# The expert stage of a graph and mixture-of-experts kernel, with TensorE's work cut into steps of one kind and two signals each

## What is computed

```python
h = (x_flat @ W_gat).reshape(M, HEADS, NUM_EXPERTS)
e = leaky_relu(a_src[src] + a_dst[dst], 0.2)
ee = exp(e - segment_max(e, dst)[dst])
agg = segment_sum(h[src] * (ee / segment_sum(ee, dst)[dst])[:, :, None], dst)
scores = layernorm(agg + b_gat).mean over heads
for ei in range(NUM_EXPERTS):            # 4
    g = weight of expert ei (softmax of the best two scores)
    hh = gelu(x @ W1[ei] + b1[ei])       # 256 -> 512
    out = out + g * (hh @ W2[ei] + b2[ei])  # 512 -> 256
```

## Time and profile before

| | us |
|---|---|
| median of 3 runs | 4049.74 (4045.44 to 4051.8) |
| the profiled execution | 4058.66, its span in the trace 4057.0 |
| PE busy over the span | 1940.2 (48%) |
| DVE busy | 1968.4 (49%) |
| ACT busy | 663.5 (16%) |
| GpSimd busy | 1737.6 (43%) |

### The profile page before, as it was taken

The page is one execution under the profiler, slowest core; times in us unless marked ns, Lnnn a source line. Parts: engine busy times, 40 slices in busy tenths (PEclk is TensorE's granted clock), DMA queues, the critical chain, the costliest instruction groups (busy, mean ns, idle before and its releaser), DMA issues.

```text
span 4057.0 us, 25978 instructions
## 1 busy us (share of the span) xinstructions
PE 1940.2 (48%) x7318; PEld 1438.6 (35%) x7322; DVE 1968.4 (49%) x3777; ACT 663.5 (16%) x1401; POOL 1737.6 (43%) x1787
## 2 busy tenths in 40 slices
PE   4415044444334353546541395554657565556425
PEld 3311033233223132324430374443546454444314
DVE  7876776645656653446520163233334343233646
ACT  7300021122112121212310011010101011011003
POOL 0015765655565444540777314344442424343241
PEclk9758566666666676767565697777878787777757
DMA  3211344544455343434621011111110111111415
GB/s 123 36 48 28 87 157 152 164 155 154 137 170 164 113 145 121 160 116 168 178 77 8 13 37 27 26 22 22 31 31 29 28 31 25 24 22 25 180 55 211
DMA packets 154183, 354.73 MB, mean 87 GB/s; under 512 B 55510, under 2 KB 96518, under 8 KB 144406
## 3 DMA queue, kind: packets, MB, share of 16 engines
q1 hardware_dynamic: 68303, 196.54, 13.5%
q0 software_dynamic: 69936, 121.07, 12.7%
q10 hardware_dynamic: 15866, 36.29, 2.3%
HBM read 181.01 MB, written 172.19 MB: 87 GB/s over the span
## 4 chain that ended last, share of the span: by engine, by line
PE 18%; another core or an unknown queue 16%; issue 10%; DVE 7%; ACT 1%; DMA 1%; POOL 0%; ACTq 0%; SPq 0%; DVEq 0%; POOLq 0%
PE ffn_psY L1512 7%; PE ffn_psH L1498 6%; PE pick_rows L858 3%; DVE pick_prod L888 1%; DVE at_ring L897 1%; DVE at_ring L692 1%; PE mid_psH L1424 1%; PE mid_psT L1181 1%; DVE pick_hot L874 0%; POOL acc L979 0%; DVE xnT L1715 0%; DVE at_high L662 0%; PE pick_node L839 0%; DVE at_ring L684 0%
## 5 line engine op out<-in xcount | busy, mean ns | idle before, releaser
L618 POOL DMA_INDIRECT at_ring<-table,e_col x768 | 725.9, 945 | 1061.2 <-DMA at_sums<-at_ring 831.2
L2057 POOL DMA_INDIRECT at_ring<-table,at_idx x693 | 671.9, 970 | 585.1 <-DMA at_sums<-at_ring 378.4
L2149 PE MATMUL at_psS<-at_ring,at_hot 128*128 128x260 f32 x1584 | 495.1, 475 | 437.4 <-issue 268.9
L1498 PE MATMUL ffn_psH<-xnT,ffn_space 128*128 x896 | 405.3, 605 | 452.5 <-ACT ffn_space L1539 289.4
L888 DVE SCALAR_TENSOR_TENSOR pick_prod<-const_iota,pick_tile,pick_rows 128x400 f32<-128x400 f16 x256 | 158.5, 629 | 831.1 <-remote 547.5
L2149 PEld LDWEIGHTS at_psS<-at_ring,at_hot 128*128 128x128 f32 x1584 | 346.9, 236 | 575.3 <-issue 351.3
L1512 PE MATMUL ffn_psY<-ffn_space 128*128 128x256 f32 x1568 | 387.7, 405 | 286.4 <-DVE ffn_space L1570 271.9
L1498 PEld LDWEIGHTS ffn_psH<-xnT,ffn_space 128*128 128x128 f32 x896 | 271.9, 312 | 553.8 <-ACT ffn_space L1539 301.0
L1512 PEld LDWEIGHTS ffn_psY<-ffn_space 128*128 128x128 f32 x1568 | 314.9, 204 | 345.8 <-DVE ffn_space L1570 285.8
L2171 ACT ACTIVATE at_ring<-at_psS 128x520 f32<-128x520 f32 (+1 forms) x432 | 238.7, 567 | 768.0 <-PE at_psS L2149 354.6
L1539 ACT ACTIVATE ffn_space<-ffn_psH,ffn_b 128x448 f32<-128x448 f32 x224 | 141.5, 634 | 1056.4 <-DMA at_sums<-at_ring 790.7
(11 more groups left out here) (404 smaller groups left out, 2432.6 us busy)
## 6 DMA issues: line engine op xcount, KB each, us to landing
at_sums<-at_ring SPq DMA_DIRECT2D x72, 1452.0 KB
products<-ffn_space ACTq DMA_DIRECT2D x28, 512.0 KB
at_ring<-table,e_col POOLq DMA_INDIRECT x867
at_sums<-at_ring SPq DMA_DIRECT2D x16, 768.0 KB, 3.2
late_space<-products SPq DMA_DIRECT2D x24, 512.0 KB, 7.9
at_ring<-table,at_idx POOLq DMA_INDIRECT x693
products<-ffn_space ACTq DMA_DIRECT2D x28, 384.0 KB
late_space<-products SPq DMA_DIRECT2D x24, 384.0 KB, 9.8
```

Of the source, the lines that this page charges most:

```text
L618: g.indirect_dma_start(self.ring[z][:, k, 0:TW], None, self.table, bass.IndirectOffsetOnAxis(ap=self.runs.col[:, u * U + k:u * U + k + 1], ...
L1498: last = pe.matmul(self.psH[part][:, 0:half], self.w1[:, k, e * HID + f:(e + 1) * HID:FT], self.xnT[:, k, bass.ds(r * (BT * P) + part * ha ...
L2057: g.indirect_dma_start(self.ring[z][:, k, 0:self.TW], None, self.table, bass.IndirectOffsetOnAxis(ap=self.idx[:, z, k:k + 1], axis=0)).the ...
L2149: last = pe.matmul(self.psS[at % 2][:, k - lo, 0:TW], self.hot[:, b, k, :], rows[:, b * self.SUB + k, 0:TW], start=True, stop=True)
```

## The change

PE's work in the stage is cut into 112 steps, 16 in a round. A step is one slice of the first layer (both parts), up to two tiles of the second layer (of the slice five steps behind, `LAG`), and two picked columns. The two tiles lie in one PSUM bank, and DVE adds the bias to both in one instruction. A step has two signals: `s_step`, on the last column, for DVE (tiles, columns and node spread together), and `s_hidden`, on the last part of the slice, for ACT. DVE does one step after one wait: `take` (mask both columns), `add`, `put` (one-hots, sum). `weigh` is cut in two pieces, placed at steps 5 and 6 for one unit and 11 and 13 for the other, `scores` at 3 and 10. The last five products of the network share their steps with further picks, and the last 5 chunks use four banks (`pick_rows` and `psH`) with one signal each. On SP, the loads of the next stage stand after the store of unit 13.

```diff
-    def column(self, pe, n, z, k, kept):
-        pe.wait_ge(self.s_kept, kept)
...
-        last.then_inc(self.s_out, 1)
+        for k in range(2):
+            pe.wait_ge(self.s_kept, r * self.ROUND + (slot * 2 + k + 1))
+            last = self.column(pe, self.ps_rows[k], i % 2, half * 2 + k)
+        return last
...
+    def hidden(self, pe, r, s):
+        e, f = divmod(s, FT)
+        for part in range(2):
+            pe.wait_ge(self.s_hid, r * (2 * self.STEPS) + (2 * s + part + 1))
...
+    def product(self, pe, r, n):
+        e, j = divmod(n % self.STEPS, FT)
+        lo, hi = self.PAIRS[j]
+        pe.wait_ge(self.s_prod, r * self.STEPS + (n + 1))
...
+        with pe.Fori(1, self.rounds) as r:
+            for s in range(self.STEPS):
+                self.product(pe, r, s - self.LAG)
+                picks(r, s).then_inc(self.s_step, 1)
+                self.hidden(pe, r, s).then_inc(self.s_hidden, 1)
...
+    def activate(self, a, r, s):
+        a.wait_ge(self.s_hidden, r * self.STEPS + (s + 1))
+        for part in range(2):
+            a.activation(self.hid[:, e % 2, f, part * half:(part + 1) * half], self.psH[part][:, 0:half],
...
+    def add(self, v, n):
+        if j % 2 == 0:
+            v.wait_ge(self.s_kept[j // 2], 16 * e + 16)
+        v.tensor_tensor(self.prod[:, lo:hi, :], self.psY[j % 2][:, 0:(hi - lo) * self.DIM].rearrange("p (t d) -> p t d", d=self.DIM),
...
-                        att.sync(sp, lambda: mix.begin(sp, ffn), ffn.rounds * 2 - 2)
+                        att.sync(sp, lambda: mix.begin(sp, ffn), ffn.rounds * 2)
...
+                        def step(i):
+                            v.wait_ge(ffn.s_step, i + 1)
+                            pick.take(v, i, pick.ps_rows)
+                            if 0 <= i - ffn.LAG < ffn.steps:
+                                ffn.add(v, i - ffn.LAG)
+                            pick.put(v, att, i)
```

More of the change, by code:

```diff
@@ L812, in table_vector @@
         v.wait_ge(self.s_att, 16)
+        v.wait_ge(self.s_node, 1)
         self.hots(v, 0)
@@ L875, in hots, with take, put @@
                 .then_inc(self.s_hot, 1)
-    def vector(self, v, att, slot):
-        q, S, D = self.q, self.SPAN, self.D
+    def take(self, v, slot, banks):
+        S, D = self.SPAN, self.D
+        tiles = self.c["iota16"][:, 0:S].unsqueeze(1).to_broadcast([P, D, S])
+        for k in range(2):
+            n = slot * 2 + k
+            v.scalar_tensor_tensor(out=self.prod[:, k, :, :], in0=tiles, scalar=self.tile[:, n:n + 1],
+                                   in1=banks[k][:, 0:S * D].rearrange("p (d s) -> p d s", d=D),
+                                   op0=ALU.is_equal, op1=ALU.mult).then_inc(self.s_kept, 1)
+    def put(self, v, att, slot):
+        q, D = self.q, self.D
         q.eng = v
@@ new lines, in hidden @@
+    def hidden(self, pe, r, s):
+        FT, K, BT, HID, half = self.FT, self.K, self.BT, self.HID, self.BT * P // 2
+        e, f = divmod(s, FT)
+        for part in range(2):
+            pe.wait_ge(self.s_hid, r * (2 * self.STEPS) + (2 * s + part + 1))
+            for k in range(K):
+                last = pe.matmul(self.psH[part][:, 0:half], self.w1[:, k, e * HID + f:(e + 1) * HID:FT],
+                                 self.xnT[:, k, bass.ds(r * (BT * P) + part * half, half)],
+                                 start=(k == 0), stop=(k == K - 1))
+        return last
@@ new lines, in product @@
+    def product(self, pe, r, n):
+        FT, DIM = self.FT, self.DIM
+        e, j = divmod(n % self.STEPS, FT)
+        lo, hi = self.PAIRS[j]
+        pe.wait_ge(self.s_prod, r * self.STEPS + (n + 1))
+        for t in range(lo, hi):
+            for f in range(FT):
+                last = pe.matmul(self.psY[j % 2][:, (t - lo) * DIM:(t - lo + 1) * DIM],
+                                 self.hid[:, e % 2, f, t * P:(t + 1) * P], self.w2[:, e * FT + f, :],
+                                 start=(f == 0), stop=(f == FT - 1))
+        return last
@@ new lines, in _ @@
+                        last = att.units - 1
+                        for i in range(ffn.steps, slots):
+                            step(i)
+                            if i == ffn.steps:
+                                att.scores(v, last - 2)
+                            if i == ffn.steps + 2:
+                                att.weigh_first(v, last - 2)
+                            if i == ffn.steps + 3:
+                                att.weigh_second(v, last - 2)
+                        chunks = range(slots // 2, pick.chunks)
@@ L2814, in _ @@
+                        for c in chunks:
+                            late_chunk(c)
+                            if c == chunks[1]:
+                                att.scores(v, last - 1)
+                            if c == chunks[2]:
+                                att.weigh(v, last - 1)
                         pick.end_vector(v)
@@ L2841, in _ @@
                         ffn.scalar(a, beside)
-                        for u in range(ffn.rounds * 2 - 1, att.units):
+                        for i in range(ffn.steps, ffn.steps + ffn.LAG + 1):
+                            ffn.store(a, 0, i - ffn.LAG - 1)
+                            if i == ffn.steps + 1:
+                                att.exponents(a, att.units - 3)
+                        for u in range(att.units - 2, att.units):
                             att.exponents(a, u)
@@ L2865, in _ @@
                     def _(pe):
-                        def between(r):
-                            pick.tensor(pe, r, next(slots))
                         join.tensor(pe)
```

235 lines of the change are left out of this document (106 added, 129 removed).

## The result

The changed kernel takes 3926.2 us (median of 4 runs, 3920.4 to 3938.2), the kernel before in the same session 4048.8: a ratio of 0.970 (95% interval 0.968 to 0.973). The forecast was 3770, with 3670 to 3900. The sign was right, and the gain is 123 us where 279 were forecast. The profiled execution took 3922.05 us, its span 3920.1.

A forecast was written before the change was run, and what follows sets the result against it. PE's signals, passing 11.2 us apart in GpSimd's gathers, were taken as the bound. Unit 3's gather at 2335 plus six rounds of 194, 56 + 73 to the last `weigh` and 149.4 gave a span of 3777, forecast 3770 us (3670 to 3900).

The forecast's parts named there:

- The bound now: Expert stage: during GpSimd's gathers PE's signals pass one at a time, in PE's order, 11.2 us each; a round takes 230.7 us.
- slow stretches: Part of each gather, from about 9 us after its start: 57 us with six signals passed, two in a round.
- a price for each signal: PE's hand-over to ACT and DVE during a gather: each signal costs 11.2 us, not a common delay.
- three places: Rival, expert-stage steps: each step takes three hand-over places, not two; a round is 209 us, the time 3895; chance 0.13.
- A round after: Expert-stage round: two stretches of 57 us pass 6 steps, the other 10 take 76, restarts 4: 194 us against 230.7.
- passes work, not signals: Rival, PE in the gathers: PE's work stalls however it is signalled; a round stays at 231, about 4030 us; chance 0.06.
- The start: First gathers up to unit 3's: unit 0 is weighed in step 13, so that gather starts at about 2335, not 2415.1.
- The end: From unit 15's gather at 3499: last `weigh` ends at 3628, 149.4 us unchanged behind it, span 3777.
- Lockstep: Rival, expert-stage steps: PE cannot run ahead, a step is 14.2 us, a round 256, about 4200 us; chance 0.07 with other new waits.
- What hides: Steps outside gathers: DVE's 5.1 us and ACT's 1.7 us a step fit beside PE's 7.6.
- the sign that had been named for an error: Profile after, DVE's masks in a gather: more than 22.4 us apart would mean three hand-over places a step and a wrong forecast.
- fewer signals made each one slower: Profile after, signals in a gather: the sign that would show the count of six signals a stretch itself wrong.

The follow-up runs named there:

- x1: Changed kernel with extra TensorE signals that nothing waits for, 100 a round as in the kernel before: 3907.1 us, 0.973 of the kernel before.
- x11: Changed kernel with GpSimd's second-attention gathers in bursts of 8 columns, each waiting for its landing: 3403.1 us, 0.848 of the kernel before in the same session.

## Why the prediction was wrong

**The bound now: right in place, wrong in kind.** The round, its two slow stretches and their 57 us were read rightly, and PE's order of hand-over too. The step that failed is the sentence "so it is a price for each signal". It was drawn from two columns and a slice part, which all have four matmuls, and the earlier trace rows with its 21.0 us for a tile of eight was kept as an oddity and made a rival ("three places") instead of a measurement of the unit. Divided by PE's matmuls in between, and the earlier trace rows give 2.8 and 2.6 us.

**A round after: 214.7 instead of 194.** The prediction let a slow stretch pass 3 whole steps, 96 matmuls, where it passes some 30 (24 by its own six signals of the earlier trace rows). With 60 matmuls handed over in the two stretches of a round, the other 452 take 108 us of the prediction's 121.9; with its 114 of stretches and 4 of restarts that is 226, hardly a gain. Of the rivals, "passes work, not signals" (0.06) comes nearest: a stretch passes a number of matmuls, however they are signalled, and signals have no price that x1 could measure. But it took PE's work for what stalls and PE's busy time in a gather as fixed. What stalls is the hand-over. PE itself went on and started 39 matmuls more in the gathers of the round shown, whose outside stretches had 6.0 us less of PE's work (92.4 to 86.4). The rest of the gain lies outside the gathers too, where PE's idle time fell from 19.3 us (111.7 - 33.9 - 58.6, rounded) to 11.0 (97.4 - 52.9 - 33.5). Over five rounds of another session the split is 9.5 and 7.0 us; which of the waits that went gives the second part was not taken apart.

**The start: 2356 instead of 2335.** The same count: step 13 takes longer if the first gathers pass matmuls. **Rounds:** five of them cost 5 x 20.7 = 103 us more than forecast, the last one (3429.8 to 3633.9) 204.1, another 10. **The end:** from unit 15's gather to the last `weigh` 137.5 us instead of 129; behind it 148.7 against 149.4. Together 21 + 103 + 10 + 9 - 1 = 142 us, and 3777 + 142 is the span of 3920 within 1.

**Lockstep** did not come: PE's idle time outside gathers fell. **What hides:** DVE's and ACT's steps did hide outside gathers, as the bursts show (142 us a round with GpSimd as the bound), and GpSimd got its buffers in time.

**The rule of the skill.** The Trainium skill (TensorE: Matmul & The Clock Gate, "The cost: per-tile semaphore tail") has a signal at 26.3 ns, which spoke against a large gain. x1 has 68 more signals a round at no measurable cost. That is compatible with the page's price (12.5 us in all, the prediction's estimate from it), but an interval of 0.5% either way, 20 us, is too wide to confirm it; the 2.80 us per matmul are another thing.

**What the profile after should have shown.** Gathers 96 to 99 and 113 to 120 us apart in turn, not 90 and 104. DVE's masks were 22 us apart from ACT's Gelus in the first two steps, as forecast, and 33.7 and 67.1 in the next: the sign that had been named for an error (over 22.4 us) was the right one, and so was the last one: fewer signals made each one slower.

## What to carry to other kernels

When an engine's results arrive at a steady distance, divide it by each thing that could be counted (signals, instructions, bytes) at two places where these differ in ratio before forecasting from one of them. If TensorE idles on its own issue while GpSimd issues gathers back to back, put short bursts with a landed wait between them: 8 columns here, 10 us, gave 15 to 18% where a new order of all of TensorE's work gave 3. Measure both kernels side by side, though: in the one session that had no slow stretches the changed kernel in these bursts was 7.5% slower than the kernel before. And a change that makes good use of a slow stretch may be worth nothing once the stretch is gone, as here, where GpSimd then sets the pace; ask first whether it can go.

## What the runs showed of the hardware

- In five of six sessions, while GpSimd issues row gathers without a pause, TensorE's matmuls are handed over ever more slowly, in the end one each 2.80 us, and TensorE's issue falls to that pace once it is far ahead. The slowing shows from some 10 to 19 us after a gather's start on and is the same with four transfers in flight. With 2 us of landing between them, bursts of 10 us leave column signals 2.4 us late at most (x11; 3.4 with bursts in both attentions), bursts of 12.5 us up to 13.1, of 15 us up to 24.6, and with 20 us most of the loss is back. What in the chip it is was not found. The runs do not tell the issue of gathers from their transfers (no run kept GpSimd busy with other work in such a session), nor a matmul from its weight load, since each has one.
- How far TensorE runs ahead can be counted in the first long gather: at 2216.2 some 16 of the 24 matmuls behind the masks of 2195.3 are not yet handed over, and 8 of columns and 7 of a product (2200 on) are started behind them, 31 or 32 in all, each with its weight load. The Trainium skill (TensorE: Matmul & The Clock Gate, "Architectural detail: the array is 16× 32×32, not 1× 128×128") gives TensorE's queue as 64 deep; with two instructions each the trace agrees.
- In one session of six the kernel before took 2755.9 us instead of 4016 to 4067, with the other kernels of that session in line. A round in bursts of 8 was 142 us there too:

```profile
2100.90:2242.90 142.00, 121.70 (x502) 104.08 (x501) 73.27 (x147) 23.90 (x37) 91.08 (x96) 0.93 0.18 38
```

  The first attention's sums had 93.3 us of idle time there with no bursts in their loop, against 427.8 in x11, and but one of 433 signals of theirs in the trace came over 0.03 us behind its matmul, so the slow hand-over was absent, not avoided. The changed kernel in bursts of 8 is then slower than the kernel before (1.075). What differs between sessions stayed open, and so did what the changed kernel would gain in such a one: it was not run there.
- A pause costs about 2 us of landing (a burst of 8 each 11.9 us, at 1.25 us a column), and one column in flight 2.7 us each (369 in 1000 us).
